# Row maxima of a causal attention: one VectorE operation per bank, or one for two neighbouring banks

## What is computed

```
q, k = rope(split(x @ Wq.T + bq)), rope(split(x @ Wk.T + bk)); v = split(x @ Wv.T + bv)
att = where(causal, q @ k.T / sqrt(16), -inf)
att = softmax(att, axis=-1)
y = (att @ v) @ Wo.T + bo
x = layernorm(x + y)
```

## Time and profile before

| | us |
|---|---|
| median of 3 runs (2768.15 to 2771.44) | 2770.11 |
| the profiled execution | 2769.75 |
| its span, first to last instruction | 2767.9 |
| busy in it: TensorE matmul | 2700.5 (98%) |
| VectorE | 1891.2 (68%) |
| ScalarE | 1353.7 (49%) |
| GpSimd | 95.3 (3%) |

### The profile page before, as it was taken

One profiled execution on the slowest core, in us unless ns is written; L12 is line 12 of the kernel. 1 busy time (PEld: TensorE's weight loads), 2 busy tenths in 40 slices (PEclk: granted clock), 3 DMA queues, 4 the chain that ended last, 5 costly groups with the idle time before them and its releaser, 6 DMA issues.

```text
span 2767.9 us, 38948 instructions
## 1 busy us (share of the span) xinstructions
PE 2700.5 (98%) x14816; PEld 1414.0 (51%) x14816; DVE 1891.2 (68%) x3938; ACT 1353.7 (49%) x2641; POOL 95.3 (3%) x174
## 2 busy tenths in 40 slices
PE   9799999999999999999999999999999999999998
PEld 5233333333333333333333332688888887888886
DVE  8899999888888888888887775533333362543343
ACT  5356666777766767777777777311111111001000
POOL 0000110001100011100000000000000000000000
PEclk9799999999999999999999999999999999999999
DMA  8721110011110011110001000411111132121100
GB/s 225 205 44 38 32 43 5 3 23 30 31 38 5 6 36 32 34 27 3 3 1 40 19 6 10 124 59 58 59 58 56 42 130 105 46 91 45 45 16 23
DMA packets 89050, 131.01 MB, mean 47 GB/s; under 512 B 26310, under 2 KB 63686, under 8 KB 85286
## 3 DMA queue, kind: packets, MB, share of 16 engines
q1 hardware_dynamic: 79068, 97.30, 11.3%
q0 software_dynamic: 6192, 22.23, 3.7%
q10 hardware_dynamic: 3616, 9.18, 1.2%
HBM read 82.46 MB, written 46.20 MB: 46 GB/s over the span
## 4 chain that ended last, share of the span: by engine, by line
PE 89%; DVE 6%; issue 2%; ACT 1%; DMA 1%; POOLq 0%; POOL 0%; ACTq 0%; DVEq 0%
PE wi_f L963 19%; PE at_o L506 18%; PE at_row L471 17%; PE at_key L485 16%; PE na_h L1181 13%; PE na_y L1193 3%; DVE at_segmax L557 3%; DVE fr_masked L553 1%; ACT at_probs L621 1%; PE at_key L488 1%; PE wi_p L808 1%; PE pr_main L125 1%; DMA pr_xt<-in_xT 1%; DVE pr_rest L219 0%; DVE pr_full L224 0%
## 5 line engine op out<-in xcount | busy, mean ns | idle before, releaser
L621 ACT ACTIVATE at_probs<-at_key 128x512 f32<-128x512 f32 (+3 forms) x2304 | 1127.1, 568 | 499.4 <-PE at_key L485 351.4
L557 DVE TENSOR_REDUCE at_segmax<-at_row 128x1 f32<-128x512 f32 x1792 | 1142.9, 684 | 167.1 <-PE at_row L471 163.0
L471 PE MATMUL at_row<-fr_k_stack,fr_q_stack 96*128 96x512 bf16 (+3 forms) x1152 | 403.7, 375 | 14.8 <-DVE at_segmax L553 10.5
L485 PE MATMUL at_key<-fr_q_stack,fr_k_stack 99*128 99x512 bf16 (+3 forms) x1152 | 414.1, 364 | 1.2 <-ACT at_probs L621 1.0
L471 PE MATMUL at_row<-at_k_stack,at_q_stack 96*128 96x512 bf16 (+3 forms) x1152 | 408.0, 364 | 1.8 <-DVE at_segmax L557 1.1
L485 PE MATMUL at_key<-at_q_stack,at_k_stack 99*128 99x512 bf16 (+3 forms) x1152 | 402.0, 364 | 7.7 <-ACT at_probs L621 7.1
L1181 PE MATMUL na_h<-fr_h,fr_h2w_h 128*128 128x512 f32 x1024 | 322.0, 396 | 1.4 <-DVE fr_h L704 1.4
L506 PE MATMUL at_o<-at_probs,fr_values 128*32 128x512 f32 (+3 forms) x2304 | 288.0, 572 | 0.0
L506 PE MATMUL at_o<-at_probs,at_values 128*32 128x512 f32 (+3 forms) x2304 | 286.9, 570 | 0.0
L553 DVE CUSTOM_DVE_ANT_0 fr_masked<-at_row,fr_causal 128x384 f32<-128x384 f32 (+3 forms) x512 | 244.0, 483 | 44.9 <-PE at_row L471 44.4
L471 PEld LDWEIGHTS at_row<-fr_k_stack,fr_q_stack 96*128 96x128 bf16 x1152 | 110.1, 98 | 310.7 <-DVE at_segmax L557 159.1
(11 more groups left out here) (120 smaller groups left out, 2466.3 us busy)
## 6 DMA issues: line engine op xcount, KB each, us to landing
hidden<-wi_h SPq DMA_DIRECT2D x64, 256.0 KB, 2.0
na_h2f<-hidden SPq DMA_DIRECT2D x8, 1024.0 KB, 7.5
q_parts<-pr_parts SPq DMA_DIRECT2D x16, 384.0 KB, 5.0
k_parts<-pr_parts SPq DMA_DIRECT2D x16, 384.0 KB, 6.8
at_q_stack<-q_parts POOLq DMA_DIRECT2D x48, 128.0 KB, 3.5
at_k_stack<-k_parts POOLq DMA_DIRECT2D x48, 128.0 KB, 3.8
outputs<-at_outs SPq DMA_DIRECT2D x128, 34.0 KB
pr_table<-in_table ACTq DMA_DIRECT2D x8, 512.0 KB, 7.6
```

What stands on the lines that cost most here:

```text
L471: last = nc.tensor.matmul(bank[:, 0:w], qst[u][0:SROWS, c, h, i * P:(i + 1) * P], kst[u][0:SROWS, h, s * CH:s * CH + w], start=True, stop= ...
L485: last = nc.tensor.matmul(bank[:, q0:CH], kst[u][0:SROWS + PARTS, h, j * P:(j + 1) * P], qst[u][0:SROWS + PARTS, c, h, q0:CH], start=True, ...
L557: nc.vector.tensor_reduce(segmax[:, n % 2, h * TPC + i, s:s + 1], row_ps[r % RING_R][:, 0:w], op=ALU.max, axis=AX.X).then_inc(rows_taken, 1)
L621: nc.scalar.activation(probs[:, g % RING_P, h, q0:CH], key_ps[m % RING_K][:, q0:CH], ACT.Exp, scale=HD ** -0.5).then_inc(probs_ready, 1)
```

## The change

- `row_pairs` goes through the list of rows and marks pairs: two neighbouring row scores of the same block, tile and head (key chunks s and s + 1), unless the first lies in the last bank of the ring. PAIRED is the number of all blocks, so pairs are taken in every one.
- The four banks of the ring become one tensor, so that an operation can read two neighbouring banks. TensorE still fills them one by one, each with its own count of rows_ready and with its wait for row r - 4.
- `segment` waits for both scores of a pair, reduces them in one operation (two maxima, or, if the second is the diagonal, one masked sum and maximum over both) and then adds 2 to rows_taken.
- A pair with the diagonal writes only one of its two places of segmax. So `clear` fills segmax with the lowest value before each block's first score, and waits for that.
- TURN_LAG goes from 4 to 8.
- The causal mask is 1024 columns wide instead of 512 (its first half zeros) and moves to the place of `x1t0`; the two masked tiles are 1024 wide.

```diff
--- before.py
+++ after.py
@@ -44,7 +44,8 @@
 TERMS = [(0, 0), (0, 1), (1, 0), (1, 1), (0, 2), (2, 0)]
 SROWS = HD * len(TERMS)
 TURN = -1
-TURN_LAG = 4
+TURN_LAG = 8
+PAIRED = NCH * NQUAD
 SLACK = 28 * CH
 FIRST_EARLY = 3
 FIRST_AHEAD = 4
@@ -285,6 +286,18 @@
     return blocks, rows, groups
 
 
+def row_pairs(blocks, rows):
+
+    firsts, r = set(), 0
+    while r + 1 < len(rows):
+        n, i, h, s = rows[r]
+        if i != TURN and n < PAIRED and rows[r + 1] == (n, i, h, s + 1) and r % RING_R != RING_R - 1:
+            firsts.add(r)
+            r += 1
+        r += 1
+    return firsts
+
+
 def row_width(c, i, s):
     return CH if s < c else (i + 1) * P
 
@@ -332,6 +345,11 @@
     out_after = {min(g + 1, NG - 1): n for n, g in last_group.items()}
     diagonal_at = [r for r, (n, i, _, s) in enumerate(rows) if i != TURN and s == blocks[n][1]]
     diagonal = {r: k for k, r in enumerate(diagonal_at)}
+    first_row = {}
+    for r, (n, i, _, _) in enumerate(rows):
+        if i != TURN:
+            first_row.setdefault(n, r)
+    paired = row_pairs(blocks, rows)
     MR = PARTS * QUAD * TPC
     PREP_QUAD = NQUAD - 1
     prep_block = blocks.index((PREP_QUAD, NCH - 1))
@@ -358,7 +376,8 @@
         maxrest = sb("maxrest", [P, QUAD * TPC])
         maxparts = sb("maxparts", [P, 2, PARTS, QUAD * TPC], BF16)
         maxrows = sb("maxrows", [MR, 2, P], BF16)
-        row_ps = [ctx.enter_context(nc.psum_tensor(f"at_row{i}", [P, CH], F32)) for i in range(RING_R)]
+        row_all = ctx.enter_context(nc.psum_tensor("at_row", [P, RING_R * CH], F32))
+        row_ps = [row_all[:, i * CH:(i + 1) * CH] for i in range(RING_R)]
         key_ps = [ctx.enter_context(nc.psum_tensor(f"at_key{i}", [P, CH], F32)) for i in range(RING_K)]
         o_ps = ctx.enter_context(nc.psum_tensor("at_o", [P, CH], F32))
 
@@ -370,6 +389,7 @@
         values_loaded = [sem(f"values_loaded{q}") for q in range(NQUAD)]
         rows_ready = sem("rows_ready")
         rows_taken = sem("rows_taken")
+        cleared = sem("cleared")
         split = sem("split")
         maxparts_ready = sem("maxparts_ready")
         max_spilled = sem("max_spilled")
@@ -545,17 +565,28 @@
             def segment(r):
 
                 n, i, h, s = rows[r]
-                w = row_width(blocks[n][1], i, s)
-                dve.wait_ge(rows_ready, r + 1)
-                if s == blocks[n][1]:
-                    if diagonal[r] >= 2:
-                        dve.wait_ge(rows_taken, diagonal_at[diagonal[r] - 2] + 1)
-                    nc.vector.tensor_tensor_reduce(out=masked[:, diagonal[r] % 2, 0:w], in0=row_ps[r % RING_R][:, 0:w], in1=causal[:, CH - w:CH],
+                c = blocks[n][1]
+                count = 2 if r in paired else 1
+                end = s + count - 1
+                w = (count - 1) * CH + row_width(c, i, end)
+                at = (r % RING_R) * CH
+                dve.wait_ge(rows_ready, r + count)
+                if end == c:
+                    k = diagonal[r + count - 1]
+                    if k >= 2:
+                        dve.wait_ge(rows_taken, diagonal_at[k - 2] + 1)
+                    nc.vector.tensor_tensor_reduce(out=masked[:, k % 2, 0:w], in0=row_all[:, at:at + w], in1=causal[:, 2 * CH - w:2 * CH],
                                                    scale=1.0, scalar=MASKED, op0=ALU.add, op1=ALU.max,
-                                                   accum_out=segmax[:, n % 2, h * TPC + i, s:s + 1]).then_inc(rows_taken, 1)
+                                                   accum_out=segmax[:, n % 2, h * TPC + i, end:end + 1]).then_inc(rows_taken, count)
                     return
-                nc.vector.tensor_reduce(segmax[:, n % 2, h * TPC + i, s:s + 1], row_ps[r % RING_R][:, 0:w],
-                                        op=ALU.max, axis=AX.X).then_inc(rows_taken, 1)
+                nc.vector.tensor_reduce(segmax[:, n % 2, h * TPC + i, s:end + 1],
+                                        row_all[:, at:at + w].rearrange("p (b t) -> p b t", b=count),
+                                        op=ALU.max, axis=AX.X).then_inc(rows_taken, count)
+
+            def clear(n):
+
+                nc.vector.memset(segmax[:, n % 2, :, :], MASKED).then_inc(cleared, 1)
+                dve.wait_ge(cleared, n + 1)
 
             def finish(n):
 
@@ -586,9 +617,11 @@
             for r, (n, i, _, _) in enumerate(rows):
                 if i == TURN:
                     take_turn(r)
-                else:
+                elif r - 1 not in paired:
+                    if r == first_row[n] and n < PAIRED:
+                        clear(n)
                     segment(r)
-                    if r == last_row[n]:
+                    if r + (r in paired) == last_row[n]:
                         finish(n)
                         if n == NB - 2:
                             prep.invert_den(dve, 0)
@@ -664,8 +697,8 @@
 
         at = 2 * STACK + VALUES
         self.x1t = [place(f"x1t{u}", at + u * X1T, [P, 2, DH, CH], F32R) for u in range(2)]
-        self.masked = place("masked", at + X1T, [P, 2, CH])
-        self.causal = place("causal", at + X1T + 2 * CH, [P, CH])
+        self.masked = place("masked", at + X1T, [P, 2, 2 * CH])
+        self.causal = place("causal", at, [P, 2 * CH])
         self.h2f = [place("h2f_a", at, [P, FK // 2, CH]), place("h2f_b", 2 * STACK, [P, FK // 2, CH])]
         at += 2 * X1T
         self.ident32 = place("ident32", at, [P, P])
@@ -1299,7 +1332,7 @@
     "x": [T, D], "xT": [NCH, P, DH, CH], "table": [NCH, P, 2, CH],
     "WqT": [D, D], "WkT": [D, D], "WvT": [D, D], "WoT": [D, D],
     "bias": [P, 2 * DH], "bv": [P, DH], "bo": [D],
-    "ident": [P, P], "mask": [P, P], "causal": [P, CH], "ones": [PARTS, QUAD * T // 2],
+    "ident": [P, P], "mask": [P, P], "causal": [P, 2 * CH], "ones": [PARTS, QUAD * T // 2],
     "w1T": [D, F], "w2T": [D, F], "h1T": [F, F], "h2T": [F, F], "w3T": [F, D],
     "s1": [P, FK], "s2": [P, FK], "hs1": [P, FK], "hs2": [P, FK], "s3": [D],
 }
@@ -1336,7 +1369,7 @@
         ones=np.full((PARTS, QUAD * T // 2), one, np.float32),
         ident=np.eye(P, dtype=np.float32),
 
-        causal=np.where(np.arange(CH)[None, :] - (CH - P) > p[:, None], MASKED, 0.0).astype(np.float32),
+        causal=np.where(np.arange(2 * CH)[None, :] - (2 * CH - P) > p[:, None], MASKED, 0.0).astype(np.float32),
         mask=np.where(p[:, None] > p[None, :], MASKED, 0.0).astype(np.float32),
     )
```

## The result

| | before | after |
|---|---|---|
| median of 4 runs each, same chip (us) | 2769.13 (2767.48 to 2771.44) | 2925.02 (2924.34 to 2926.62) |
| the profiled execution; its span | 2769.75; 2767.9 | 2925.09; 2923.2 |
| instructions on VectorE | 3938 | 3066 |

The account below looks back on a forecast made before the run. The prediction took TensorE as the bound, VectorE holding it up only in some early and middle blocks. To 2769.75 us it added 102.8 - 7 + 10 + 0 + 11 + 0.6 = 117, giving 2887 us, range 2812 to 2945.

Parts of the forecast that it names:

- 102.8 - 7: Blocks 5 to 10 and 12 to 28: 229 late rows cost 102.8 us, less 7 us these blocks already lose.
- The mechanism: In groups opening on a pair's second row, TensorE's row score waits for the pair's joint release: 102.8 us in 229 cases.
- The twenty waits in a row: Blocks 23 and 7: a row matmul waits 0.4 us once a group, twenty groups running; about 98 us, not 89.
- Fill to release: Ring, issue of a pair's second row to its release: 0.43 + 1.22 + 0.05 = 1.70 us.
- Blocks 0 to 4 and 11: Late rows set against waits already there: +10 us in blocks 1 to 4, 0 in block 11, 0 in block 0.
- The clear: Memset of segmax once a block on VectorE, 0.4 us for 28 blocks: +11 us (0 to 25).
- The later turn: Turns four scores later, with their matmuls, copies and DMAs: cost 0, as covered; without cover 2.8 us a block.
- VectorE's saving: Pair operations on VectorE: 0.067 us a pair, 61 us of busy time; nothing gained where TensorE is the bound.
- Smaller stalls: Rival: some late rows fall where TensorE would wait anyway; 15% to 60% of 103 us, 2785 to 2846; chance 0.06.
- A second start within the pair: Rival: the pair operation takes 1.28 to 1.37 us, not 1.22, in 277 cases; 2904 to 2929 us; chance 0.09.
- The clock: Rival: TensorE's clock falls in stalls, once per block for 24 blocks; +41 us, 2928; chance 0.09.
- Faster, and without effect: Two rivals: VectorE's saving decides, 2763 us, chance 0.07; the change cancels or does not act, 2770 us, chance 0.03.

Follow-up runs that it names:

- x1: The changed kernel with PAIRED = 0, so no pairs and no clear; the later turn, joined tensor and wider mask stay: 2763.18 us, 0.9982 of before.
- x5: The changed kernel with only the 637 of 904 pairs that make no row late, clear kept: 2782.52 us, 1.0045 of before.
- x4: The changed kernel, each pair taken by two single operations that both wait for the second score, released jointly: 2926.26 us, 1.0568 of before.
- x12: The changed kernel with pairs and clear only in the rows of block 23: 2769.75 us, 1.0006 of before.
- x3: The changed kernel, each score of a pair reduced by itself once filled, both banks still released together: 2809.30 us, 1.0145 of before.
- x6: The changed kernel with only the 680 pairs of two full chunks, diagonals single, no clear: 2885.75 us, 1.0415 of before.
- x7: The changed kernel without pairs but with the clear of segmax in every block: 2774.57 us, 1.0013 of before.
- x2: The changed kernel with TURN_LAG back from 8 to 4, all pairs kept: 2940.72 us, 1.0613 of before.
- x8: The changed kernel with only 511 pairs, of full chunks and making no row late, and no clear: 2770.18 us, 1.0004 of before.
- x10: The kernel before with TURN_LAG 8 instead of 4 and nothing else: 2762.39 us, 0.9978 of before.
- x11: The kernel before with TURN_LAG 12 instead of 4: 2760.08 us, 0.9965 of before.
- x9: The changed kernel, a full pair's reduce reading 1024 columns as one row and writing one maximum: 2927.82 us, 1.0571 of before.

## Why the prediction was right or wrong

The profiled executions, grouped by the forecast's terms (us, cut at the copies of the blocks' outputs; block 0 from 110 on):

| blocks | before | x1 | after | after - before | forecast |
|---|---|---|---|---|---|
| 5 to 10, 12 to 28 | 1293.0 | 1290.8 | 1410.9 | +117.9 | 102.8 - 7, and 9 of the clear |
| 1 to 4 | 176.6 | 173.3 | 202.1 | +25.5 | +10, and 2 |
| 11 | 61.1 | 61.5 | 67.2 | +6.1 | 0 |
| 0 | 46.6 | 45.9 | 52.2 | +5.6 | 0 |

**The mechanism was right.** The waits are at row scores, released by VectorE's pair; the blocks with many groups that open on a pair's second row are 11 to 12.5 us longer (23, 7, 5), block 24 6.4; blocks 14 to 17 are unchanged (0.4 us at most); the feed-forward too. x5 shows that the pairs that make a row late carry nearly all of it, x4 that the joint operation is not needed for it, and x12 that the loss is local. The twenty waits in a row that were forecast for blocks 23 and 7 are 20 in each. The time missed by 38 us of 156 all the same, and 2925 alone could not have told the forecast from two of its rivals (2904 to 2929, and 2928).

**Fill to release was mis-sized: 1.77 us, not 1.70.** The step took the way to VectorE, 0.43 us, from a single reduce. Over all reduces of after that a row score released, the median is 0.49 us for 1024 columns (307 cases) and 0.42 for 512; before it is 0.43 (292 cases). By x3 this goes with the release of 2, not with the columns. The 1.22 us were right, by the slope of the masked sum. With 0.07 more in 229 cases: 102.8 + 16.0 = 118.8 us. Measured in these blocks: after against x1 120.1, less the clear's 4.0 there, so 116.1. That this is so close is in part luck. The price takes 0.218 us for every matmul in between, but those on the diagonal are narrower. With each at its own width the same 229 cases sum to some 130 us (an estimate from the code), from which the 7 us already lost may go off. And the count that the expectation of x6 names, 198 us for all 302 cases, stands against 162, the clear's 11 among them.

**Blocks 0 to 4 and 11 were mis-sized: +37 us where some 12 stood.** There the step set the late rows' price against the wait that stood there already, as if they overlapped. Nearer to the runs is that they add up: against x1, blocks 1 to 4 are 28.8 us longer and block 11 5.7, where the cases there come to 32.5 and 4.5 by the same prices with 1.77. In block 0, put at 0, the code has 17 late rows, and 6.3 us are seen. Adding up would follow if a late row makes VectorE, the bound there, late with its next scores; no run tried it. The clock is a part of it. A finish in the stretch of block 1 of after, in order of time:

```profile
169.22 0.17 DVE L604 TENSOR_TENSOR at_maxparts<-at_maxrest,at_maxparts 128x16 bf16<-128x16 f32 x1
169.37 0.17 DVE L588 MEMSET at_segmax<- 128x128 f32 x1
...
169.63 1.22 DVE L582 TENSOR_REDUCE at_segmax<-at_row 128x2 f32<-128x1024 f32 x1
...
170.91 0.61 PE L491 MATMUL at_row<-fr_k_stack,fr_q_stack 96*128 96x512 bf16 x1 [1.86 <-DVE at_segmax L582]
```

Finish, memset and the first pair leave TensorE idle for 1.86 us, and the next matmul takes 0.61 us where others take 0.39. A block's stretch times what its clock lacks of 1.00, times two, is its time at 1.2 GHz: in block 1 9.9 us against 3.6 before, in block 11 6.7 against none, in block 2 none against 3.2. At half speed at most half of such time is lost, so these three lose up to 5 us more than before. How the other 32 us divide between waits added up and the chain at the finish stays open.

**The clear** cost what was forecast (11, measured 11.4), but by luck: the forecast had put 9 of it in the blocks bound by TensorE. In the traces of x7 and x1 those differ by 4.0 us and blocks 0 to 2 by 11.2, of 16.1 in all. The lower clock there is a part of it in this one execution; how large a part in the others is open. The cover that the forecast worked with rests on a short reading, too: the finish takes 0.98 us until the next reduce starts (202.67 to 203.65), not 0.89, which is the way to its last step's start.

**The later turn** was put at 0 and gives 6 us without pairs, 15.7 with them. The step looked only at what the later turn might delay, for which it had cover, and not at what it takes away: TensorE's wait at the turn's matmul, which stands at L465 in the rows of waits above (9.4 us in 12 waits). Not all of it is gained: row scores wait 8.1 us in 15 waits behind reduces in x1, 3.3 in 11 before. With the turn left at four the change would have cost 171 us (x2).

**VectorE's saving** was 61 us of busy time by forecast. Busy time fell by 39.4, or 45 with the memsets' 5.3 set aside: 0.05 us a pair, not 0.067; why is open. As argued, it buys nothing: x8 has 21 us less than x1 and is 7 slower. By the 125 ns an instruction on PSUM of the Trainium skill, "Perfetto Trace Analysis", section "Optimizing Scalar/DVE Operations", it would have been 113 us, an estimate; the measurement decides.

**The rivals.** Smaller stalls, 15% to 60% of the 103 us: refuted by 116 us in those blocks. (Its times didn't fit together: 2785 leaves the other terms of the sum out, 2846 has them in.) A second start within the pair: refuted by 1222 ns, though a later start of 0.06 to 0.07 stood in its place. The clock: not in the stalled groups, block 23 and 24 stay at 1.00 through twenty and eleven stalls; but the rival's place, the finish, was right for early blocks. The Trainium skill, "TensorE: Matmul & The Clock Gate", section "A second HAM failure mode: psum-queue depth-cycling", tells of a clock that goes up and down where TensorE pauses between groups of matmuls; for pauses of 0.3 to 0.7 us once a group these runs don't bear it out. Faster, and without effect: refuted. The Trainium skill, "Perfetto Trace Analysis", section "Optimizing Scalar/DVE Operations", says that breaking instructions up may help where VectorE isn't saturated but causes bubbles. Here that holds: of the two ways to take the same 1024 columns, the one in single steps (x1) is 162 us faster, the clear's 11 among them.

## What to carry to other kernels

In a ring, ask when a bank comes free, not how long the engine is busy: to join two operations means to begin with the second input and to release with the end of both, and with four banks and a row every 0.44 us that was 1.77 us against the 1.31 in which TensorE came back. Some 0.06 of it came with giving back two banks by one addition of 2. Price it by counting from the program's order where a row meets it; with 1.77 in it two ways of counting came out 2% and some 12% above what was measured in the blocks bound by TensorE. Here a result that goes back to the bottleneck (the turned maxima) was better taken up later than it was ready: moving the turn four scores further, alone, gave 6.7 us (x10), and eight gave 9.0 (x11). It was the only part of the change worth keeping.

## What the runs showed of the hardware

- A reduce of two neighbouring PSUM banks (1024 columns) that adds 2 to a semaphore starts 0.49 us after the last matmul's issue, one of a bank that adds 1 or nothing 0.42 or 0.43. It is not the length, nor the second bank, nor the second maximum: a reduce of one bank that adds 2 starts at 0.50 (x3). In these traces an operation that adds 2 has its wait in an instruction of its own ahead of it.
- The masked sum of 1024 columns takes 1221 ns and the reduce 1222, against 683 and 684 at 512; a maximum more costs nothing (x9: 1222).
- TensorE's granted clock in the first blocks differs between kernels that differ little: in block 1 it is 1.00 in x1, 0.84 in x7 with one memset of 165 ns a block more, but 1.00 again in x5 with the same memset, and 0.94 in x12, which does there what x1 does. Block 1 takes 27.9 us in x1 and 32.1 in x7. A single profiled execution doesn't show that the memset is the cause.
